# Group 0 with x rows stationary, smaller first loads, and another order of the small sums, in a float32 matrix product with relu and residual

## The reference

```python
hidden = jnp.concatenate([cond_512, cond_512], axis=-1)
x_mean = jnp.mean(x, axis=1, keepdims=True)
fused = jnp.concatenate([x, x_mean * ones_L, hidden[:, None, :] * ones_L], axis=-1)
return x + jax.nn.relu(jnp.einsum('bld,do->blo', fused, W) + b)
```

## Time and profile before

| | us |
|---|---|
| median of 3 runs | 104.72 (104.24 to 104.89) |
| the profiled execution | 105.41 |
| its span in the profile | 103.3 |
| TensorE busy | 96.9 (94%) |
| VectorE busy | 80.9 (78%) |
| ScalarE busy | 47.3 (46%) |
| GpSimd busy | 41.5 (40%) |
| mean DMA rate | 206 GB/s, 21.4 MB |

### The profile page before, as it was taken

The page is one execution under the profiler, slowest core; times in us unless marked ns, Lnnn a source line. Parts: engine busy times, 40 slices in busy tenths (PEclk is TensorE's granted clock), DMA queues, the critical chain, the costliest instruction groups (busy, mean ns, idle before and its releaser), DMA issues.

```text
span 103.3 us, 1722 instructions
## 1 busy us (share of the span) xinstructions
PE 96.9 (94%) x523; PEld 78.2 (76%) x523; DVE 80.9 (78%) x146; ACT 47.3 (46%) x116; POOL 41.5 (40%) x37
## 2 busy tenths in 40 slices
PE   5959999999999999999999999999999999999940
PEld 2339999778888786888888886888888868888930
DVE  3173578999899999999999966999999976557630
ACT  3267335795508379497396002973951007310000
POOL 1029700000000003999846501488485089992000
PEclk9999999999999999999999999999999999999999
DMA  2999999999999997999999595000780870595994
GB/s 61 293 300 261 234 233 238 268 274 249 268 296 232 251 226 222 254 244 274 303 331 293 154 229 162 0 0 0 181 226 0 210 196 1 171 290 132 251 309 168
DMA packets 35439, 21.39 MB, mean 207 GB/s; under 512 B 2021, under 2 KB 33129, under 8 KB 35433
## 3 DMA queue, kind: packets, MB, share of 16 engines
q1 hardware_dynamic: 33848, 20.13, 78.9%
q10 hardware_dynamic: 1584, 1.18, 4.3%
HBM read 12.91 MB, written 8.39 MB: 206 GB/s over the span
## 4 chain that ended last, share of the span: by engine, by line
PE 89%; ACTq 4%; ACT 2%; issue 0%; DVE 0%
PE ps_y L459 76%; PE ps_y L560 4%; PE ps_y L562 4%; PE ps_y L561 4%; ACTq L168 2%; ACTq L158 2%; PE ps_mean L478 1%; PE ps_const L527 1%; ACT xh L259 1%; ACT w1h L252 1%; ACT L244 0%; DVE w L449 0%; PE ps_y L583 0%; ACT act_warm L244 0%
## 5 line engine op out<-in xcount | busy, mean ns | idle before, releaser
L234 POOL TENSOR_TENSOR xa<-xa,back 128x512 f32 x28 | 36.1, 1314 | 45.1 <-DVE back L346 45.1
L459 PE MATMUL ps_y<-xh,w1h 128*128 (+2 forms) x128 | 43.9, 370 | 1.1 <-ACT w1h L252 1.1
L459 PE MATMUL ps_y<-xl,w1h 128*128 (+2 forms) x128 | 43.0, 363 | 0.0
L459 PE MATMUL ps_y<-xh,w1l 128*128 (+2 forms) x128 | 42.9, 363 | 0.0
L259 ACT ACTIVATE xh<-ps_xt 128x512 fp32r<-128x512 f32 (+1 forms) x36 | 19.8, 550 | 19.4 <-DVE ps_xt L333 19.4
L459 PEld LDWEIGHTS ps_y<-xh,w1h 128*128 128x128 f32 x128 | 22.6, 188 | 6.7 <-ACT xh L259 1.6
L339 DVE TENSOR_TENSOR xl<-ps_xt,xh 128x512 fp32r<-128x512 f32 (+1 forms) x36 | 22.2, 618 | 4.7 <-ACT xh L259 4.7
L333 DVE STREAM_TRANSPOSE ps_xt<-xa 128x512 f32<-128x512 f32 (+1 forms) x36 | 22.3, 642 | 4.5 <-DMA xa<-in_x_dram 4.2
L459 PEld LDWEIGHTS ps_y<-xh,w1l 128*128 128x128 f32 x128 | 22.6, 189 | 3.8
L459 PEld LDWEIGHTS ps_y<-xl,w1h 128*128 128x128 f32 x128 | 22.7, 189 | 3.5
L277 ACT ACTIVATE relu_t<-ps_y,bias 128x512 f32<-128x512 f32 x20 | 13.5, 686 | 16.7 <-DVE bias L380 15.3
(11 more groups left out here) (34 smaller groups left out, 34.1 us busy)
## 6 DMA issues: line engine op xcount, KB each, us to landing
xa<-in_x_dram SPq DMA_DIRECT2D x60, 128.0 KB, 4.3
out_dram<-xa SPq DMA_DIRECT2D x28, 256.0 KB, 4.1
w<-in_L_cond_W_dram SPq DMA_DIRECT2D x4, 256.0 KB, 6.2
w<-in_L_cond_W_dram SPq DMA_DIRECT2D x2, 512.0 KB, 6.9
w<-in_x_dram SPq DMA_DIRECT2D x4, 256.0 KB, 3.9
out_dram<-w SPq DMA_DIRECT2D x3, 256.0 KB, 3.3
xa<-in_x_dram ACTq DMA_DIRECT2D x4, 128.0 KB, 4.2
w<-in_L_cond_W_dram SPq DMA_DIRECT2D x4, 64.0 KB, 3.2
```

The source lines that it names most:

```text
L234: nc.gpsimd.tensor_tensor(rows, rows, back[:, t], ALU.add).then_inc(added, 1)
L459: return nc.tensor.matmul(ps_y[:, t, ls], lhs, rhs, start=start, stop=stop, skip_group_check=True)
```

## The change

Group 0 is computed like the last group: 128 rows of x stationary, W1's columns streaming, first the row blocks 0 and 1 as their pieces of 128 columns come, then blocks 2 and 3. Its x comes in parts of 128, 128 and 256 rows; the first two parts, and W1's first two slices, in loads of 64 KB. `w1_high` is halved, with VectorE copying the other half (`w1_rest`). SyncE alone loads W1's second half and x's third part, then x of group 1, then cond, b, x of group 2 and W2 in two halves.

Group 0's output lies in rows: ScalarE copies it to W1's room (`save_first`), and later GpSimd adds the bias row, ScalarE takes the relu, and GpSimd adds x, which is loaded again in rows (`first_x`). These stand between the tiles 9 to 18 by `BIAS_AT`, `RELU_AT`, `X0_AT`. The tile numbers n now begin with group 1, so there are 24 turned back. Six tiles are saved ahead of the bias instead of eight.

`mean_terms(1)` stands ahead of the addition of cond's product, with two rooms for `w2x` and two PSUM banks; TensorE's `mean_bias(0)` and `(1)` come inside group 2, `(2)` in group 4's last tile, `(3)` behind group 6's third. On VectorE `sum_bias(2)` stands ahead of tile 9's turning back, `sum_bias(3)` ahead of tile 20's. The bias of batch 0 goes through DRAM by SyncE, that of batch 3 by ScalarE's queue, each with one store of four partitions. Warm-up products: 10 instead of 14. `relu_done` and `y_saved` give way to a common count `y_free`.

```diff
-WARM = 14
+WARM = 10
...
+    PARTS = ((0, P), (P, P), (2 * P, 2 * P))
+    FIRST = ((0, 0), (0, 1), (0, 2), (1, 0), (1, 1), (0, 3), (1, 2), (1, 3)) + tuple((2, k) for k in range(NK))
+    pieces = [(0, *PARTS[part], k) for part, k in FIRST]
...
+    tiles = [(g, t) for g in range(1, LAST) for t in range(NK)]
+    SAVED = NK + 2
...
+    X_FROM, X_BEHIND = 0, 3
+    def has_x_step(n, shift=0):
+        return 0 <= n - X_FROM - shift < NK * (G - SLOTS)
+    BIAS_AT, RELU_AT, X0_AT = (9, 10, 11, 12), (13, 14, 15, 16), (12, 13, 17, 18)
 
...
             load_x0(sp, 0, LOW)
             load_w1(sp, 0, 1, LOW)
+            load_x0(sp, 1, LOW)
             load_w1(sp, 1, 2, LOW)
-            load_w1(sp, 2, NK, LOW)
-            load_x0(sp, 1, LOW)
+            load_w1(sp, 2, NK, ORDER)
+            load_x0(sp, 2, ORDER)
+            load_x(sp, 1, ORDER)
             sp.wait_ge(cond_zeroed, 1)
             for j in range(NQ):
                 sp.dma_start(cond_c[Q * j:Q * j + B], cv[j].rearrange("b (m k) -> b m k", k=CK)).then_inc(cond_landed, 16)
-            load_x(sp, 1, ORDER)
-            load_x(sp, 2, ORDER)
-            load_w2(sp, ORDER)
             for j in range(NQ):
                 sp.dma_start(b_row[Q * j:Q * j + Q], bvec[P * j:P * j + P].partition_broadcast(Q)).then_inc(b_landed, 16)
+            load_x(sp, 2, ORDER)
+            for k in range(0, NK, NK // 2):
+                load_w2(sp, k, k + NK // 2, ORDER)
             load_x(sp, 3, ORDER)
             for r in range(2):
                 sp.dma_start(w3[:, r], w3v[r]).then_inc(w3_landed, 16)
-            for g in range(SLOTS, G):
-                load_x(sp, g, ORDER)
+            load_x(sp, 4, ORDER)
+            load_x(sp, 5, ORDER)
+            sp.wait_ge(bias_summed, 1)
+            store_bias(sp, 0, 0)
+            load_x(sp, 6, ORDER)
+            sp.wait_ge(bias_stored, 16)
+            sp.dma_start(last_bias[:], bias_line[0].partition_broadcast(P)).then_inc(last_bias_landed, 16)
+            load_x(sp, 7, ORDER)
+            sp.wait_ge(xt_ready, pieces_to(1))
+            for r in range(NR):
+                sp.dma_start(first_x[:, r], x_rows[0, :, r]).then_inc(first_x_landed, 16)
             sp.wait_ge(const_summed, 1)
             for r in range(NR):
                 sp.dma_start(last_x[:, r], x_rows[LAST, :, r]).then_inc(last_x_landed, 16)
-            for g in range(LAST):
-                if g == LAST - 2:
-
-                    sp.wait_ge(bias_summed, B)
-                    for j in range(NQ):
-                        sp.dma_start(bias_line[P * j:P * j + P], bias_row[Q * j + B - 1]).then_inc(bias_stored, 16)
-                    sp.wait_ge(bias_stored, 16 * NQ)
-                    sp.dma_start(last_bias[:], bias_line.partition_broadcast(P)).then_inc(last_bias_landed, 16)
-                sp.wait_ge(added, NK * (g + 1))
...
+                if g == LAST - 3:
+                    for r in range(NR):
+                        sp.wait_ge(first_added, r + 1)
+                        sp.dma_start(out_rows[0, :, r], first_x[:, r]).then_inc(stored, 16)
...
+            for n, (g, t) in enumerate(tiles):
+                residual(g, t, n + 1)
+                if n in BIAS_AT:
+                    r = BIAS_AT.index(n)
+                    pool.wait_ge(y_free, r + 1)
+                    pool.wait_ge(last_bias_landed, 16)
+                    nc.gpsimd.tensor_tensor(first_y[:, r], first_y[:, r], last_bias[:], ALU.add).then_inc(first_biased, 1)
+                if n in X0_AT:
+                    r = X0_AT.index(n)
+                    pool.wait_ge(first_relu_done, r + 1)
+                    pool.wait_ge(first_x_landed, 16 * NR)
+                    nc.gpsimd.tensor_tensor(first_x[:, r], first_x[:, r], first_y[:, r], ALU.add).then_inc(first_added, 1)
...
+            def save_first(r):
+                act.wait_ge(y_ready, r + 1)
+                act.wait_ge(w1l_ready, r + 1)
+                nc.scalar.activation(first_y[:, r].rearrange("p (j t m) -> p t j m", j=NQ, t=NK),
+                                     ps_y[:, r].rearrange("p (t j m) -> p t j m", t=NK, j=NQ), ACT.Copy).then_inc(y_free, 1)
...
+                if n == NK * (LAST - 2):
+                    act.wait_ge(bias_summed, B)
+                    store_bias(act, 1, B - 1)
+                elif n == NK * (LAST - 2) + 1:
+                    act.wait_ge(bias_stored, 16 * 2)
+                    act.wait_ge(first_biased, NR)
+                    act.dma_start(last_bias[:], bias_line[1].partition_broadcast(P)).then_inc(last_bias_landed, 16)
+                if has_x_step(n, X_BEHIND - X_FROM):
                     x_high(n_x)
                     n_x += 1
+                if n in RELU_AT:
+                    r = RELU_AT.index(n)
+                    act.wait_ge(first_biased, r + 1)
+                    nc.scalar.activation(first_y[:, r], first_y[:, r], ACT.Relu).then_inc(first_relu_done, 1)
...
+            def w1_rest(k):
+                dve.wait_ge(w1_landed[min(k, NK - 2)], 16 * NQ)
+                nc.vector.tensor_copy(as_tiles(w1h[:, k])[:, DVE_T:NK], by_tile(w1[:, k])[:, DVE_T:NK]).then_inc(w1h_rest_ready, 1)
...
             turn_x(0)
-            turn_and_split(0, pieces_to(1))
+            turn_x(1)
+            w1_rest(0)
+            x_low(0)
+            turn_x(2)
+            x_low(1)
+            turn_x(3)
+            x_low(2)
+            turn_x(4)
+            x_low(3)
+            w1_rest(1)
+            turn_x(5)
+            x_low(4)
+            turn_x(6)
+            x_low(5)
+            turn_x(7)
+            w1_rest(2)
+            x_low(6)
+            w1_rest(3)
+            x_low(7)
+            turn_x(8)
+            turn_and_split(8, pieces_to(1))
+            turn_x(pieces_to(1))
+            turn_and_split(pieces_to(1), pieces_to(H))
 
             dve.wait_ge(cond_landed, 16 * NQ)
             nc.vector.transpose(cond_t[:], cond_c[:].rearrange("p m k -> p k m")).then_inc(cond_spread, 1)
-            turn_x(pieces_to(1))
-            turn_and_split(pieces_to(1), pieces_to(H))
             turn_x(pieces_to(H))
             turn_and_split(pieces_to(H), pieces_to(H + 1))
             mean_terms(0)
             n_x = pieces_to(H + 1)
             turn_x(n_x)
             turn_and_split(n_x, n_x + NK)
+            mean_terms(1)
             dve.wait_ge(const_summed, 1)
             dve.wait_ge(b_landed, 16 * NQ)
             nc.vector.tensor_tensor(const_row[:], ps_const[:, 0:P], b_row[:], ALU.add).then_inc(const_ready, 1)
             dve.wait_ge(const_ready, 1)
             sum_bias(0)
-            mean_terms(1)
+            sum_bias(1)
             n_x = pieces_to(SLOTS)
             for n in range(len(tiles)):
-                if n == 2:
-                    sum_bias(1)
-                elif n == NK * (H + 1):
+                if n == 2 * NK + 1:
                     sum_bias(2)
-                elif n == NK * H * (B - 1):
-                    sum_bias(B - 1)
+                elif n == 5 * NK:
+                    sum_bias(3)
                 turn_back(n)
-                for _n in range(steps_of_x(n, 3)):
-                    if n % NK == 0:
+                if has_x_step(n):
+                    k = (n - X_FROM) % NK
+                    if k == 0:
                         turn_x(n_x)
-                    if n % NK < NK - 1:
+                    if k < NK - 1:
                         turn_x(n_x + 1)
                     x_low(n_x)
                     n_x += 1
-                if n // NK + SLOTS - 1 < G and n // NK > 0 and n // NK % H == 0 and n % NK == NK - 1:
-                    mean_terms(n // NK // H + 1)
-            dve.wait_ge(last_bias_landed, 16)
+                    if pieces_to(SLOTS + H) == n_x:
+                        mean_terms(2)
+                    elif pieces_to(SLOTS + 2 * H) == n_x:
+                        mean_terms(3)
...
+            def first_rows(k, r, x, w, start=False, stop=False):
+                return nc.tensor.matmul(ps_y[:, r], x[:, 0, k, P * r:P * r + P], w[:, k], start=start, stop=stop, skip_group_check=True)
+            def first_low(k, stop=False):
+                pe.wait_ge(w1l_ready, k + 1)
+                for r in (0, 1):
+                    last = first_rows(k, r, xh, w1l, stop=stop)
+                    if stop:
+                        last.then_inc(y_ready, 1)
+            for k in range(NK):
+                pe.wait_ge(w1h_ready, k + 1)
+                pe.wait_ge(w1h_rest_ready, k + 1)
+                for r in (0, 1):
+                    piece = FIRST.index((r, k))
+                    pe.wait_ge(xh_ready, piece + 1)
+                    first_rows(k, r, xh, w1h, start=(k == 0))
+                    pe.wait_ge(xl_ready, piece + 1)
+                    first_rows(k, r, xl, w1h)
+                if k == 0:
+                    first_low(0)
+                elif k > 1:
+                    first_low(k - 1)
+            first_low(NK - 1, stop=True)
+            for k in range(NK):
```

(77 more changed lines are left out.)

184 lines of the change are left out of this document (93 added, 91 removed).

## The result

| | before | changed |
|---|---|---|
| median, us | 104.53 (104.24 to 104.89, 4 runs) | 110.32 (109.92 to 110.80, 4 runs) |
| the profiled execution | 105.41 | 110.58 |
| its span | 103.3 | 108.1 |

The ratio is 1.055, with an interval of 1.051 to 1.059. The direction was forecast, the size not: 5.8 us, where I had 1.7 and a range up to 107.9.

The account below looks back on a forecast made before the run. TensorE was taken to bound the kernel, with GpSimd and the stores a second bound at the end. GpSimd's end of 95.45 - 93.52 - 0.27 = 1.66 us later gave 104.72 + 1.7 = 106.4 us, range 103.7 to 107.9.

Parts of the forecast that it names:

- GpSimd's end: GpSimd's last addition, group 6: forecast to end at 95.45 against 93.52, with the stores following it.
- the start of the busy stretch: Tile 9's turning back, forecast at 64.6; from there GpSimd owes 23 instructions at 1.25 us, 28.75 us.
- GpSimd's rest at the sums: GpSimd empty from 80.9 until tile 16 is turned back at 82.4, behind batch 3's sums: 1.6 us (0 to 2.9).
- contention at the tail: GpSimd's last additions running into VectorE's instructions at the end: 0.5 us (0 to 1).
- The 0.27: At the end: the time TensorE could gain before the stores bound it, subtracted from GpSimd's delay.
- 0 to 2.5 at the sums, which I leave to the range: Batch 3's sums on VectorE, blocked by GpSimd's additions: 0 to 2.5 us, left to the range.
- Rival C: Batch 3's sums lose each turn to queued GpSimd, tile 16 turned back 1.5 us later: 107.9 us; chance 0.17.
- the head start: Kernel start: first product 1.5 us sooner at 5.7, 0.6 left at group 1 (18.3), about 1.0 at group 2.
- the stall of 0.8: Ahead of group 5: TensorE idle 0.8 us until the relu behind `sum_bias(2)`, at 64.7.
- D: Head start eaten by the starved two-row phase, TensorE loses 1 us, stores keep 106.4; chance 0.38 together with the forecast.
- A: GpSimd keeps up, ends by 93, and TensorE's lead of 0.9 shows: 103.8 us; chance 0.21.
- B: Even: GpSimd ends between 93 and 94.8, stores absorb TensorE's lead: 104.0 to 105.7 us; chance 0.24.

Follow-up runs that it names:

- GpSimd yields: Changed kernel with GpSimd waiting ahead of tile 14's residual until VectorE has done batch 3's sums: 110.64 us, ratio 1.060.
- the changed one with its tail on VectorE: Changed kernel with tiles 26 and 27 of group 6 turned back into PSUM and added by VectorE: 109.58 us, ratio 1.047.

## Why the prediction was right in direction and wrong in size

**The spans add up.** Forecast: GpSimd's end at 95.45, 1.93 us later than before, of which 1.66 reach the time. Measured: 98.26, and a span 4.8 longer. Of the difference to 95.45, 0.26 us is the start of the busy stretch (64.86 instead of 64.6), 2.0 GpSimd's rest at the sums (3.60 instead of 1.6), 0.43 contention at the tail (0.93 instead of 0.5), 0.12 that the 23 additions took 28.87 instead of 28.75: 2.81. The 0.27 that I took off for the stores was no saving, since the 9.8 us behind their start are the time in which the last two megabytes drain, eight blocks of 256 KB. 1.66 + 2.81 + 0.3 = 4.8. The medians differ by another 1.0: some 0.4 lie around the span (110.58 - 108.1 = 2.5, before 2.1), and 0.6 is where the profiled executions lie to their medians.

**The step that failed** is "0 to 2.5 at the sums, which I leave to the range": a mechanism that I had named, with its row, was entered in the sum at nothing. It measured 2.5 us on one instruction (2.63 against 0.14). The five sums took 5.43 us, where the forecast had 3.5, the old kernel's 78.56 to 82.06. Rival C said it, with its condition, two additions waiting, and that was the case in the trace: 78.67, x2. Tile 16 came 1.64 us after my 82.4, where C had 1.5. C's 107.9 was still too low because it kept my tail, my start and the 0.27, and because of the 1.0 between the medians, which no forecast of mine had. When my own text says that VectorE's chain is without rest and that GpSimd will have no rest there either, the likeliest value of their contention isn't zero. The range had the same fault: its upper end was one rival's middle.

**Point by point.** First product 5.7: measured 5.50. x of group 2 turned at 22.1: 22.08. Bias 0 at 40.8: bias rows at 40.79. First subtraction of group 4 at 44.1: 44.37. Sums for batch 2 at 56.9: 57.19. `sum_bias(2)` at 63.4: 63.56. Tile 9's residual at 64.6: 64.86. Contiguous additions at 1.29: 1.30. Last subtraction of x at 78.3: 78.04. The counting of issues and steps along VectorE's chain held to 0.3 us over 60 us. Part of that is luck: in two other kernels that are the same up to there, GpSimd yields and the changed one with its tail on VectorE, tile 9's residual starts at 65.73 and 66.03.

Wrong was the head start. Group 1 at 18.3 was 18.5 to 19.3 in eight runs of the new head, where the old head has 18.65 to 18.99. Its 1.7 us at the first product don't reach group 1: the second pair waits for x, slice 2 for its load. Nor does what is left reach the end. TensorE begins group 7 at 87.91, before at 87.92; in the eight runs of the new head at 87.82 to 89.05, in the four of the old at 87.30 to 87.92. In the five other profiles of the new head in which the clock held and that are used to their end, TensorE stood 0.3 to 0.8 us near 41 us for cond's row and 0.2 to 0.4 ahead of group 5 for a relu; in the changed kernel, with its products later, neither occurred, so the stall of 0.8 that I had forecast ahead of group 5 wasn't there. So D was the case: the head start isn't there, and GpSimd and the stores held the end. A and B fell with GpSimd's end. The last bias landed near 92.3 instead of 90.4, without cost, since VectorE was held up by the ring until 92.48. With GpSimd out of the way VectorE did wait for it (1.95 us without the additions, 2.24 with them moved), but TensorE's products ran on without a gap.

What stays open: what lowered the clock at the start (below), for which nothing was varied but the number of warm-up products; and whether the new head could pay with W1's second half loaded sooner, which wasn't tried.

## What to carry to other kernels

GpSimd's additions and VectorE's instructions with two SBUF inputs are one resource: before you give GpSimd more work, lay both engines' busy stretches over each other, and price the overlap at whole instructions of the other engine, for as many as are queued. The order of waits that was tried here didn't help; moving work to where the other engine rests did, and so did an operand in PSUM.

At the end of a kernel, count the stores behind the last one that waits, and how long these drain: work that ends sooner pays only if its bytes leave sooner too. The cheapest gain here was two residuals on VectorE, which sent a megabyte off 2.8 us sooner.
